# Where the branch stands: spreading root steps, scaled rows and splits over an attention loop, and moving TensorE's choice of body

## The reference, cut to what matters

```python
deg = jnp.clip(adj.sum(axis=1), 1.0)
dis = deg ** (-0.5)
adj_norm = dis[:, None] * adj * dis[None, :]
diffusion = adj_norm @ x - x
norms = jnp.maximum(jnp.linalg.norm(x, axis=-1), COS_EPS)
sim = x @ x.T / (norms[:, None] * norms[None, :])
attn = jax.nn.softmax(beta * sim * adj, axis=1)
return diffusion + jax.nn.sigmoid(alpha) * (attn @ x - x)
```

## Time and profile before

| what | value |
|---|---|
| median of 3 runs | 649.95 us (647.13 to 650.79) |
| the profiled execution | 648.9 us |
| its span, first to last instruction | 647.1 us |
| busy: TensorE, VectorE, ScalarE, GpSimd | 87%, 77%, 65%, 62% of the span |
| mean granted TensorE clock | 0.947 of full |

### The profile page before, as it was taken

How to read it: one execution, slowest core, us unless ns; L and a number is a source line. 1 busy time by engine, 2 the same in 40 slices (tenths; PEclk the granted TensorE clock), 3 DMA queues, 4 the chain that set the end, 5 groups by cost and what they waited for, 6 DMA issues and landing times.

```text
span 647.1 us, 11836 instructions
## 1 busy us (share of the span) xinstructions
PE 561.2 (87%) x4145; PEld 346.3 (54%) x4145; DVE 496.8 (77%) x985; ACT 419.7 (65%) x713; POOL 403.8 (62%) x463
## 2 busy tenths in 40 slices
PE   0899999899898979997539898899999999969993
PEld 0555555343344868886538553444444444448882
DVE  3777877987996644788787867899998999985452
ACT  3888777699996614689966237787877888850000
POOL 6798887699998154556104235687777788204663
PEclk9899999999999689999558999999999999978997
DMA  7999985000000000000000121333332233000100
GB/s 128 107 109 108 108 298 189 1 1 1 2 0 7 1 8 24 21 18 10 18 1 26 54 81 48 95 95 90 90 101 64 81 104 95 24 5 18 29 26 17
DMA packets 19929, 37.23 MB, mean 58 GB/s; under 512 B 2586, under 2 KB 11054, under 8 KB 19854
## 3 DMA queue, kind: packets, MB, share of 16 engines
q0 software_dynamic: 7392, 24.32, 20.9%
q1 hardware_dynamic: 12462, 11.98, 5.6%
HBM read 48.72 MB, written 10.45 MB: 91 GB/s over the span
## 4 chain that ended last, share of the span: by engine, by line
PE 54%; DVE 21%; ACT 12%; issue 8%; POOL 1%; DVEq 1%; DMA 1%; SPq 1%; POOLq 0%; ACTq 0%
PE PSALL L1949 9%; PE PSALL L1573 8%; PE PSALL L1628 7%; PE PSALL L1641 6%; PE PSALL L1848 5%; DVE ring L1439 4%; DVE ring L1432 4%; PE PSALL L1777 3%; ACT AW L721 3%; PE PSALL L1908 3%; ACT ring L641 3%; PE PSALL L1618 2%; ACT PSALL L646 2%; PE PSALL L1609 2%; DVE FR L1439 2%
## 5 line engine op out<-in xcount | busy, mean ns | idle before, releaser
L444 POOL TENSOR_TENSOR R<-R,ring 128x452 f32<-128x452 f32 (+2 forms) x126 | 144.9, 1170 | 20.4 <-ACT ring L641 17.1
L1573 PE MATMUL PSALL<-XN 128*128 128x452 f16 (+2 forms) x396 | 97.8, 357 | 5.9 <-DVE ring L1022 5.8
L641 ACT ACTIVATE ring<-ring,sm 128x452 f32<-128x452 f32 (+1 forms) x132 | 86.9, 661 | 20.1 <-DVE ring L1022 19.8
L1848 PE MATMUL PSALL<-AW,R 128*128 128x452 fp8e4 (+1 forms) x348 | 77.5, 354 | 16.6 <-DVE R L1371 10.3
L1022 DVE TENSOR_TENSOR ring<-PSALL,AT 128x452 f32<-128x452 f32 (+1 forms) x132 | 81.0, 618 | 10.8 <-PE PSALL L1573 9.3
L505 POOL DMA_INDIRECT AW<-ATd,FR x44 | 56.1, 1276 | 32.5 <-DVE FR L1322 17.8
L1029 DVE TENSOR_TENSOR AW<-PSALL,ring 128x452 bf16<-128x452 f32 (+2 forms) x106 | 65.3, 617 | 8.4 <-ACT PSALL L646 8.1
L1908 PE MATMUL PSALL<-ring,XW 128*128 128x452 bf16 (+1 forms) x300 | 67.7, 360 | 1.0 <-DVE ring L1439 1.0
L1573 PEld LDWEIGHTS PSALL<-XN 128*128 128x128 f16 (+1 forms) x396 | 36.6, 97 | 53.7 <-DVE ring L1022 14.5
L646 ACT ACTIVATE PSALL<-ring 128x452 f32<-128x452 f32 (+2 forms) x106 | 58.4, 551 | 9.6
L1628 PE MATMUL PSALL<-ring,AO 128*128 128x452 bf16 (+2 forms) x220 | 62.3, 364 | 1.9 <-DVE AW L1029 1.7
(11 more groups left out here) (280 smaller groups left out, 1065.6 us busy)
## 6 DMA issues: line engine op xcount, KB each, us to landing
AT<-in_adjT POOLq DMA_DIRECT2D x22, 338.5 KB, 35.2
ATd<-AT SPq DMA_DIRECT2D x2, 3723.5 KB, 17.4
X<-in_x SPq DMA_DIRECT2D x2, 704.0 KB, 6.1
XWd<-ring SPq DMA_DIRECT2D x11, 128.0 KB, 1.8
out<-ring SPq DMA_DIRECT2D x21, 64.0 KB, 1.5
AW<-ATd,FR POOLq DMA_INDIRECT x44, 4.3
X<-XWd,idx POOLq DMA_INDIRECT x22, 2.5
Wt<-in_W SPq DMA_DIRECT2D x1, 64.0 KB, 3.2
```

The lines of the kernel that those rows point to most:

```text
L444: i = G.tensor_tensor(ES_, ES_, z, ALU.add)
L641: S.activation(z, z, ACT.Exp, scale=bcol[0:rows, :]).then_inc(s_exp, 1)
L1573: m = TE.matmul(PSALL[0:rows, b, 0:w], lh[:, jt * P:jt * P + rows], rh[:, c0:c0 + w], start=(k == 0), stop=(k == 2))
L1848: TE.matmul(PSALL[:, b, 0:w], den_h[:, s + 1 + q, :, part], AW[:, jt % 3, q, c0:c0 + w], start=(q == 0 and part == 1), stop=False)
```

## The change

On VectorE, `roots` becomes five pieces, one in each of units 73 to 77. On ScalarE, the scaled rows begin at unit 79 and come in every second unit, to unit 121; the high parts are made when the last tile of their group is scaled, at units 90, 102, 114 and 122, and VectorE's low parts three units later. On GpSimd, the splits of chunks 3 to 5 and a small memset go from behind the choice to the end of the attention's body. On TensorE, the wait for the flag, its load and the branch come ahead of the transposes `turn`, which stand in both bodies now; the body for a large beta comes first and the usual one last; tile 0 of `spread` leaves the body and stands in the common loop.

```diff
-        ROOTS, XD, HIGH, LOWS = NH + 4, NH + 10, NH + 34, NH + 38
+        ROOTS, XD = NH + 4, NH + 13
+        HIGH = [XD + 2 * (t0 + nt) - 1 for t0, nt in SL]
+        LOWS = [u + 3 for u in HIGH]
...
                     if u in SPLIT:
                         sums_parts(SPLIT[u])
+                for c in range(HC, NC):
+                    sums_parts(c)
+                G.memset(AOT[:, N:NP], 0.0).then_inc(s_pad, 1)
...
-            for c in range(HC, NC):
-                sums_parts(c)
-            G.memset(AOT[:, N:NP], 0.0).then_inc(s_pad, 1)
...
-                    if not shifted and 0 <= u - XD < T:
-                        scaled_rows(u - XD, 1)
-                    if not shifted and 0 <= u - HIGH < 3 * len(SL) and (u - HIGH) % 3 == 0:
-                        scaled_high((u - HIGH) // 3)
+                    if not shifted and 0 <= u - XD < 2 * T and (u - XD) % 2 == 0:
+                        scaled_rows((u - XD) // 2, 1)
+                    if not shifted and u in HIGH:
+                        scaled_high(HIGH.index(u))
...
-            def roots():
-
-                dv.wait_ge(s_dis, 3)
-                dv.wait_ge(s_up, 1)
-                k = own.step(V.tensor_tensor(cs, root0, root0, ALU.mult))
-                dv.wait_ge(own.sem, k)
-                k = own.step(V.tensor_tensor(cs, cs, dis, ALU.mult))
-                dv.wait_ge(own.sem, k)
-                k = own.step(V.tensor_scalar(cs, cs, -0.5, 1.5, ALU.mult, ALU.add))
-                dv.wait_ge(own.sem, k)
-                k = own.step(V.tensor_tensor(dis, root0, cs, ALU.mult))
-                dv.wait_ge(own.sem, k)
-                V.tensor_scalar(dup, dis, up_x, None, ALU.mult).then_inc(s_dis, 1)
+            def roots(n):
+
+                if n == 0:
+                    dv.wait_ge(s_dis, 3)
+                    dv.wait_ge(s_up, 1)
+                    own.step(V.tensor_tensor(cs, root0, root0, ALU.mult))
+                    return
+                dv.wait_ge(own.sem, own.n)
+                if n == 1:
+                    own.step(V.tensor_tensor(cs, cs, dis, ALU.mult))
+                elif n == 2:
+                    own.step(V.tensor_scalar(cs, cs, -0.5, 1.5, ALU.mult, ALU.add))
+                elif n == 3:
+                    own.step(V.tensor_tensor(dis, root0, cs, ALU.mult))
+                else:
+                    V.tensor_scalar(dup, dis, up_x, None, ALU.mult).then_inc(s_dis, 1)
...
-                    if u == ROOTS + 3:
-                        roots()
-                    if not shifted and 0 <= u - LOWS < 3 * len(SL) and (u - LOWS) % 3 == 0:
-                        scaled_low((u - LOWS) // 3)
+                    if 0 <= u - ROOTS - 3 < 5:
+                        roots(u - ROOTS - 3)
+                    if not shifted and u in LOWS:
+                        scaled_low(LOWS.index(u))
...
-            turn(0)
-            turn(1)
+            def turns():
+
+                turn(0)
+                turn(1)
...
-                spread(0)
...
             pe.wait_ge(s_flag, 1)
             beta_large = eng.value_load(flag[0:1, 0:1], min_val=0, max_val=1)
             met = pe.covered()
-            with eng.If(beta_large == 0):
-                attention(False)
+            with eng.If(beta_large == 1):
+                turns()
+                attention(True)
             pe.only(met)
             with eng.Else():
-                attention(True)
+                turns()
+                attention(False)
             pe.only(met)
...
-                if it:
-                    spread(it)
+                spread(it)
```

More of the change, by code:

```diff
@@ L1556, in turn @@
                 m.then_inc(s_xnT, 1)
-            turn(0)
-            turn(1)
[L1560 to L1567, removed]
+            def turns():
+                turn(0)
+                turn(1)
+                pe.wait_ge(s_pm, 1)
+                TE.transpose(PSALL[0:1, 5, 0:P], pm, ident[:, :]).then_inc(s_scale, 1)
+                turn(2)
+                turn(3)
+                pe.wait_ge(s_top, 1)
+                TE.matmul(PSALL[:, 5, 0:1], orow, top, start=True, stop=True).then_inc(s_scale, 1)
+                turn(4)
+                turn(5)
             def logits(jt, c, b):
```

## The result

| | before | after |
|---|---|---|
| median | 650.12 us (12 runs) | 656.17 us (12 runs, 652.16 to 657.28) |
| the profiled execution, its span | 648.9, 647.1 us | 654.08, 652.3 us |
| mean granted TensorE clock | 0.947 | 0.959 |

The ratio is 1.0095, with a 95% interval of 1.0073 to 1.0118: 6.05 us slower, above the upper end of the range, 651.5. In what follows each ratio goes by the kernel before as timed together with that kernel, which is why its median changes a little from one experiment to the next; places of instructions come from one profiled execution of each kernel.

What follows compares the result with a forecast made beforehand. Bound: VectorE's late x preparation at the start, TensorE to unit 66, ScalarE at units 76 to 97, then TensorE. Sum 2.7 - 1.3 - 3.2 = -1.8 us on 649.95 gives 648.1 us; range 644.7 to 651.5.

Steps and rivals of the forecast that it cites:

- The start's loss, 2.7 us: At the start, TensorE's flag wait, load and taken branch put its first transposes at 18.03 instead of 15.36.
- the price of the branch, 3.56 us: At the start, the jump to the usual body costs what the taken branch cost at the old body's end.
- a sign of being wrong: At the start, the prediction is wrong if TensorE's first transposes stay before 16 us or come after 20.
- Rival 3: At the start, the code fetch waits behind queued adjacency loads; with 18 packets ahead +4.9 us, 654.9 us; chance 12%.
- Nothing comes back for the old choice: Before unit 0, the old choice cost nothing on the path, TensorE waiting for VectorE there anyway; 0 us returned.
- The second half, 1.3 us: Attention units 66 to 131: spread roots and rows every second unit gain 1.3 us, bounds 0 and 2.8.
- the lower bound: Second half: gain 0 if root steps always meet GpSimd's adds and unit 125's low part stalls TensorE's tail.
- rival 4: The second half gives nothing, ScalarE remaining the bound and the last low part late; -0.5 us, 649.5 us; chance 15%.
- The end, 3.2 us: Attention's end: jump gone, transposes at full clock, earlier GpSimd splits gain 3.2 us, bounds 2.5 and 5.
- the step that answers to 216.59: Attention's end: VectorE's step, waiting 0.28 us for ScalarE's scaling of x by the gate, moves to about 213.3.
- the one of 220.45: Attention's end: VectorE's step starts at 216.75, 3.7 us sooner, VectorE no longer waiting for TensorE there.
- TensorE's wait of 3.00: After the attention's end, TensorE's 3.00 us wait before 229.43 grows by about 1.2; longer idle may lower the clock.

Runs made afterwards that it cites:

- the moved code: The changed kernel with 32 more transposes in the large-beta body, which does not run, so the usual body's code lies further on; 650.72 us, ratio 1.003.
- the kernel with the early flag and held loads: The changed kernel with VectorE writing the flag before its sums of squares and the adjacency loads held until these are done; 646.28 us, ratio 0.9962.
- the one with TensorE as before: The changed kernel with TensorE's program as it was before the change, the other engines keeping theirs; 648.79 us, ratio 1.0005.
- the last kernel of the experiments: The changed kernel with the flag written before the sums of squares, adjacency loads held until these are done, and TensorE's program as before; 648.34 us, ratio 0.9985.

## Why the prediction was wrong

**The start's loss, 2.7 us, was mis-sized; it measured 8.7.** The step that failed is the price of the branch, 3.56 us from the earlier trace rows. That row has idle DMA queues; the new branch is issued at 14.4, when the loads have been going out since 8.77. The first transposes then stand at 18.03 + 6.26 - 3.56 = 20.73, which is where they are (20.72), so flag, load and the rest of that sum were right; they came after 20, which the prediction had named as a sign of being wrong. The loads as the cause are shown: without them the same branch took 3.36 us. A second term was missing: the next part of the code, awaited for 2.75 us. Its dependence on the code's place is shown by the moved code, its dependence on the loads by the 0.83 with the loads held. The remaining 8.7 - 5.4 - 2.75 = 0.6 was not pursued.

Rival 3, at 12%, had the cause, the loads beside the branch, and its 654.9 us missed by only 1.3. That nearness is luck. It needed at least 14 packets of 0.37 us ahead of one branch; the branch was 2.7 us longer, some seven packets' worth. Another 2.75 came from a second wait that it didn't have, and the first pass and layer 1, of which it said nothing, moved by 1.5 and 2.7 us the one way and the other. My reason against it, that instructions have a queue of their own, is no protection: the page of the profile lists the queue, and what is moved through it still took 2.9 us longer. In how the loads delay it the rival isn't borne out: a wait behind everything that was queued would have grown between the branches at 9.9 and 20.8 us, and it didn't. How the code shares the DMA engines with the loads, these runs don't tell.

The Trainium skill, "Runtime: NRT & Kernel Launch", Instruction fetch mechanics, has both halves of this: a taken branch out of the window waits for a fetch, which all of the long branches agree with, and crossing into the next block is called mostly hidden, which does not hold here right behind a branch with loads in the queues (2.75, 3.85 and 4.16 us). No run shows where one block ends and the next begins.

**Nothing comes back for the old choice.** It cost nothing on the path, as said. But what the start loses was not passed on whole to unit 66: 1.5 us came back in the first pass. Before has a stretch at half clock there, 26.0 to 29.4 us, and after has none. I had looked for a wait for adjacency tiles and not for the clock, so this is a term left out. The price of the stretch holds in the others: 99.5 us in the kernel with the early flag and held loads, which has no such stretch, and 101.1 in the one with TensorE as before and the one with the roots whole, which have it. But that the change took the stretch away isn't shown. The kernels with the roots whole and with rows in every unit have, up to unit 73, the same program as the one with the early flag and held loads, and yet they have the stretch and it has not; and the last kernel of the experiments, which has TensorE as before, has none (99.5 us).

**The second half, 1.3 us, measured 1.0, but not by its reasons.** Of the 1.3, 0.6 less 0.3 were put down to the roots and VectorE's parts and 1.0 to the rows. The roots brought nothing: the five steps took 2.8 us in one piece and 3.5 spread out, where the sum had 2.4. Two of them were long, the last scalar one among them. Single lines of the kernel after:

```profile
L979 DVE TENSOR_TENSOR st<-st x1: 1149/1149/1149, 132.1 to 132.1; 128x22 f32<-128x22 f32 x1
...
L989 DVE TENSOR_SCALAR st<-st,sm x1: 1206/1206/1206, 138.3 to 138.3; 128x22 f32<-128x22 f32 x1
```

I had 0.2 for the latter. And GpSimd, "hidden" by the prediction, was not quite: its adds have 25.6% of the chain of waits from 108 to 235 us after, where they had 5.1%, and halving them gave 1.1 us, in the way said above. The chain by line, kernel after, then before:

```profile
by line: POOL R L446 25.6%; issue 11.7%; ACT ring L643 11.2%; ACT PSALL L648 8.7%; PE PSALL L1580 8.1%; PE PSALL L1635 7.0%; DVE AO L1106 3.1%; DVE AO L1102 2.6%; POOL AW L433 2.5%; ACT R L620 2.5%; PE PSALL L1625 2.1%; PE PSALL L1647 2.0%;
```

```profile
by line: ACT ring L641 13.2%; PE PSALL L1573 12.1%; PE PSALL L1628 10.9%; issue 10.1%; ACT PSALL L646 10.0%; PE PSALL L1641 8.6%; ACT R L618 5.5%; POOL R L444 5.1%; PE PSALL L1618 4.0%; DVE ring L1022 2.8%; PE PSALL L1736 2.2%; DVE AO L1101
```

The reason that I gave for the lower bound, root steps that meet GpSimd's adds, was thus right for the roots; rival 4, which gave the whole second half nothing, was not.

**The end, 3.2 us, measured 3.5.** Here the steps held: no gap and the full clock behind tile 0; the splits behind the last add; the step that answers to 216.59 came 219.81 - 211.83 = 8.0 us behind the last copy, forecast 213.3 - 205.5 = 7.8; the one of 220.45 waits for nothing and came 11.3 behind it, where it was 14.85; and TensorE's wait of 3.00 grew to 4.00 (forecast by 1.2). One reason was wrong: not ScalarE's scaling is late next (it starts at 215.49, 3.7 behind the last copy, forecast 4.4) but the row sums, which waited 1.18 us for GpSimd's last split, and VectorE then behind them. GpSimd's adds ended only 0.4 us before the last copy, where it was 0.8 before. That the step came out within 0.2 us of the forecast, by another wait, is luck.

**The sum had no term for layer 1.** After loses 2.1 us more between layer 1's first weighted sums and its output products. The single line of those sums, before and, in the second fence, after:

```profile
L1848 PE MATMUL PSALL<-AW,R x348: 350/353/368, 372.7 to 565.5; 128*128 128x452 fp8e4 x145, 128*128 128x448 fp8e4 x29
```

```profile
L1855 PE MATMUL PSALL<-AW,R x348: 350/353/582, 375.2 to 569.7; 128*128 128x452 fp8e4 x145, 128*128 128x448 fp8e4 x29
```

The longest product shows it: 368 ns means that no product ran at half clock, 582 that some did, and it takes 194.5 us from first to last instead of 192.8. That is 1.7 of the 2.1. Of the others only the kernel with just the flag early (367 ns, 192.9 us) and the one with the loads held until the transposes (367, 192.8) are free of it. All the rest have it, the fastest one too, with the early flag and held loads (580, 194.5). The one with TensorE as before (586, 196.0) lost more here than it had gained: 2.7 us ahead at the first sums, 1.0 behind at the output products. In its profiled execution that is where the gains at the attention's end went. What decides whether the clock falls in this stage was not settled, and with one profile of each kernel it isn't shown that the change caused this loss. Nor was the difference between the profiles and the medians (5.2 and 6.05 us) settled.

## What to carry to other kernels

Take a jump's price from a place with the same DMA traffic, and count a second wait for code behind it too: here 3.3 to 3.8 us on idle queues, 5.9 to 6.4 beside bulk loads, and up to 4.2 more right behind it. If a choice has to be made at the start, make it before the bulk loads are issued and hold them for it: that turned a loss of 0.95% into a gain of 0.4% with the same jump. A microsecond saved ahead of a stage whose clock may fall is not yet a microsecond of the kernel; measure it at the end.

## What the runs showed of the hardware

The far branch took 5.88 to 6.40 us wherever it was issued, at 9.9, 14.1 to 14.8 or 20.8 us, as long as the adjacency loads were in the queues, and 3.34 to 3.82 us without them, at the start (3.34, 3.36, 3.60, 3.82) as well as at the attention's end (3.52, 3.56, 3.80). Behind it TensorE can stop again for code, by where that code lies (2.75 us against none with 32 transposes put ahead of it). A scalar step over 128x22 took 1.21 us beside GpSimd's adds, as long as a step with two tensors (1.15). With the adds halved the two took 0.26 and 0.16 us, another step still 0.67. The Trainium skill, "SBUF — State Buffer", Who interferes with whom, says that a VectorE instruction with both inputs in SBUF contends with GpSimd's reads through the port pair that the two share, and that tensor_scalar can contend in the modes that use both ports; the two rows agree.
